# Vision tower kernel: part of VectorE's set-up stands behind the first pixel sums

## The reference

```
x_new = s*x - dt*s*a*z + dt*s*Bu
z_new = dt*s*x + s*z + dt*dt*s*Bu
```

## Time and profile before

| | us |
|---|---|
| median of three runs | 881.12 |
| the three runs | 879.34, 881.12, 882.15 |
| the profiled execution | 881.01 |
| its span in the trace | 879.2 |

### The profile page before, as it was taken

How to read it: one execution, slowest core, us unless ns; L and a number is a source line. 1 busy time by engine, 2 the same in 40 slices (tenths; PEclk the granted TensorE clock), 3 DMA queues, 4 the chain that set the end, 5 groups by cost and what they waited for, 6 DMA issues and landing times.

```text
span 879.2 us, 23479 instructions
## 1 busy us (share of the span) xinstructions
PE 838.2 (95%) x9144; PEld 360.6 (41%) x9144; DVE 717.9 (82%) x1189; ACT 483.5 (55%) x782; POOL 524.4 (60%) x387
## 2 busy tenths in 40 slices
PE   5799999999999999999999997898999999999996
PEld 2134334344344343343343443464444444444442
DVE  5788888888888888888888888894788788788785
ACT  3646456455454464564554554358666566566562
POOL 2699999999999999999999964101121121121110
PEclk9999999999999999999999998999999999999999
DMA  9588998989989989999899764000000000000000
GB/s 374 158 240 252 260 283 245 263 267 260 275 250 260 286 242 259 278 250 263 256 253 264 217 168 111 2 2 2 0 13 13 25 13 13 25 13 13 25 13 36
DMA packets 70560, 141.60 MB, mean 161 GB/s; under 512 B 5440, under 2 KB 5440, under 8 KB 69440
## 3 DMA queue, kind: packets, MB, share of 16 engines
q1 hardware_dynamic: 70464, 140.21, 55.4%
HBM read 68.88 MB, written 4.19 MB: 83 GB/s over the span
## 4 chain that ended last, share of the span: by engine, by line
PE 39%; POOL 37%; issue 7%; DVE 7%; ACT 4%; DMA 3%; SPq 2%; POOLq 1%; DVEq 0%; ACTq 0%
POOL sb_rows L497 11%; POOL sb_prodv L604 7%; POOL sb_rows L502 6%; PE ring L1207 5%; POOL sb_wgt L592 4%; PE ring L1177 4%; POOL sb_rows L504 3%; POOL sb_score L586 3%; PE ring L952 3%; PE bank_ms L1219 3%; DMA sb_wbc<-sb_wgt 3%; SPq L545 2%; PE bank_ms L924 2%; PE qp L991 2%; PE qp L1162 2%
## 5 line engine op out<-in xcount | busy, mean ns | idle before, releaser
L952 PE MATMUL ring<-sb_arena,sb_wqkv 64*64 64x512 f32 x2048 | 254.1, 599 | 2.3 <-DVE sb_prodk L1349 1.5
L1380 DVE TENSOR_TENSOR sb_prodv<-ring,sb_wbc 128x1024 f32<-128x1024 f32 x128 | 151.8, 1206 | 43.6 <-DMA sb_wbc<-sb_wgt 25.4
L1349 DVE TENSOR_TENSOR sb_prodk<-ring,sb_qbuf 128x1024 f32<-128x1024 f32 x128 | 150.6, 1218 | 22.3 <-PE ring L952 16.8
L648 POOL TENSOR_TENSOR sb_parts_q<-sb_arena,sb_const 128x512 fp32r<-128x512 f32 x15 | 15.6, 1039 | 245.6 <-DVE sb_arena L1585 194.4
L497 POOL TENSOR_TENSOR sb_rows<-sb_arena 128x2048 f32<-128x2048 f32 x31 | 142.2, 4586 | 15.8 <-DVE sb_sum L489 15.8
L692 ACT ACTIVATE sb_xsq<-sb_arena 128x2048 f32<-128x2048 f32 x64 | 118.6, 1901 | 2.0 <-DMA sb_arena<-x 2.0
L952 PEld LDWEIGHTS ring<-sb_arena,sb_wqkv 64*64 64x64 f32 x2048 | 66.3, 132 | 115.6 <-issue 72.3
L991 PEld LDWEIGHTS qp<-sb_prodv,sb_tok_w 64*64 64x64 f32 x3072 | 93.1, 137 | 40.4 <-issue 40.2
L991 PE MATMUL qp<-sb_prodv,sb_tok_w 64*64 64x128 f32 x3072 | 98.8, 276 | 5.2 <-POOL sb_prodv L604 5.2
L604 POOL TENSOR_TENSOR sb_prodv<-sb_prodv 128x256 f32<-128x256 f32 x128 | 92.8, 735 | 10.7 <-DVE sb_prodv L1380 10.7
L663 ACT ACTIVATE sb_means<-sb_sum 128x256 f32<-128x256 f32 x32 | 13.3, 416 | 146.9 <-POOL sb_sum L507 143.1
(11 more groups left out here) (248 smaller groups left out, 1450.1 us busy)
## 6 DMA issues: line engine op xcount, KB each, us to landing
sb_arena<-x SPq DMA_DIRECT2D x64, 1024.0 KB, 7.4
sb_wbc<-sb_wgt SPq DMA_DIRECT2D x256, 256.0 KB, 5.7
out<-sb_arena SPq DMA_DIRECT2D x16, 256.0 KB, 2.0
sb_rest_w<-rest_w SPq DMA_DIRECT2D x1, 950.5 KB, 21.3
sb_const<-const SPq DMA_DIRECT2D x1, 264.5 KB, 3.0
sb_tok_w<-tok_w SPq DMA_DIRECT2D x1, 260.5 KB, 2.9
sb_const<-const SPq DMA_DIRECT2D x1, 256.0 KB, 21.6
```

The costliest lines, as they stand in the source:

```text
L952: mm = pe.matmul(ring[slot][C * half:C * half + C, i, :], image_block(w, i), x[C * i:C * i + C, m, half, c], start=True, stop=True)
L1349: dve.tensor_tensor(by_pixel(prodk[:, c]), by_pixel(ring[c % 2][:, :, :]), q[:, :, None, :].to_broadcast([P, 2, N_PIX, G32]), ALU.mult).th ...
L1380: dve.tensor_tensor(prodv[:, :, :, G32 * c:G32 * (c + 1)], by_pixel(ring[k % 2][:, :, :]), by_pixel(wbc[:, c]), ALU.mult).then_inc(values_ ...
```

## The change

On DVE, `double_steps(1)` and `double_steps(2)` stay where they are. `double_steps(4)`, `double_steps(8)` and the six small operations go from in front of the two bias operations to behind the second half of the first pixel sums. Nothing is added or taken out, and no other engine's program changes.

```diff
-            for k in (1, 2, 4, 8):
+            for k in (1, 2):
+                double_steps(k)
+            dve.wait_ge(setup_mm, 2)
+            dve.tensor_copy(bqkv[:, 1:2], banks[1][:, 1:2]).then_inc(biases_ready, 1)
+            dve.tensor_scalar(bqkv[:, 0:1], banks[1][:, 0:1], float(C) ** -0.5, None, ALU.mult).then_inc(biases_ready, 1)
+
+            first_patch_sums(dve, 0)
+            dve.wait_ge(setup_mm, 3)
+            dve.tensor_tensor(bqkv[:, 2:3], banks[2][:, 0:1], vec(V_PROJB), ALU.add).then_inc(weights_scaled, 1)
+            first_patch_sums(dve, 1)
+
+            for k in (4, 8):
                 double_steps(k)
             link(dve.tensor_scalar(svc(SV_F), svc(SV_S), DT * DT, None, ALU.mult))
             link(dve.tensor_tensor(svc(SV_FB), svc(SV_F), vec(V_BB), ALU.mult))
...
             link(dve.tensor_scalar(svc(SV_G), svc(SV_S), 1.0, None, ALU.add))
             link(dve.tensor_tensor(svc(SV_G), svc(SV_G), svc(SV_NM), ALU.add))
             assert n_coefs[0] == N_COEFS
-            dve.wait_ge(setup_mm, 2)
-            dve.tensor_copy(bqkv[:, 1:2], banks[1][:, 1:2]).then_inc(biases_ready, 1)
-            dve.tensor_scalar(bqkv[:, 0:1], banks[1][:, 0:1], float(C) ** -0.5, None, ALU.mult).then_inc(biases_ready, 1)
-
-            first_patch_sums(dve, 0)
-            dve.wait_ge(setup_mm, 3)
-            dve.tensor_tensor(bqkv[:, 2:3], banks[2][:, 0:1], vec(V_PROJB), ALU.add).then_inc(weights_scaled, 1)
-            first_patch_sums(dve, 1)
```

## The result

| | before | changed |
|---|---|---|
| median of 15 runs, us | 880.80 | 884.42 |
| lowest and highest | 878.81 to 882.73 | 880.96 to 890.60 |
| profiled execution, us | 881.01 | 885.80 |
| its span | 879.2 | 884.0 |

The ratio is 1.0047, with a 95% interval of 1.0032 to 1.0062: the kernel became slower by 0.47%, where 0.3% faster was forecast. Ratios and their intervals aren't quotients of medians (1.0041 here) and can differ from them by about 0.001. The changed kernel also scatters more, over 9.6 us against 3.9.

A forecast was written before the change was run, and what follows sets the result against it. In the first 36 us the filling of the pipeline counts, with DVE's set-up the path; later PE and POOL are near full. From span 879.20, minus 2.68, plus 1.81, rebased to the median: 878.4; eight in ten 876.7 to 880.6.

The forecast's parts named there:

- What comes forward on DVE: DVE's set-up and first pixel sums: L1318 starts at 7.77, L483 waits for data until 8.00; sums 2.68 us earlier.
- rival (b): Transfers of x are the limit: landing 1 us later loses 0.8 to 1.0, giving 879.3; chance 0.12.
- The place is an idle stretch of 3.12 us, the block is 2.77, so it costs nothing: Behind DVE's pixel sums: moved block runs 13.43 to 16.20, hidden by the wait for ACT, 0.36 to spare; nothing charged.
- POOL wins 0.8 and it costs nothing downstream: POOL's first instruction, limited by unit 1's second half landing at 15.5, gains 0.8 us; its reader ACT isn't delayed.
- TensorE's clock: PE's slow first pixel-mean matmuls: stretch moved, not changed, taken as 0; bounds 0.36 won or 1.3 lost.
- Rival (c): PE stays at the low rate from its new start to unit 1's squares: loss 6.7, ending at 885.1; chance 0.03.
- All behind 27 us is the same sequence, displaced: Behind 27 us no clock of its own is left: everything follows 2.68 us earlier, full stages neither stretching nor absorbing it.
- Rival (d): Moved block on DVE isn't hidden, later slots late by 0.36 and again 1 us: 879.4; chance 0.05.

The follow-up runs named there:

- experiment 5: Changed kernel, with DVE's six small operations also waiting for unit 1's pixels, as POOL's first instruction does, tensor inputs kept: 886.54, ratio 1.0072.
- 6: Changed kernel, DVE's six small operations also wait for unit 1's pixels; FB, CD and G take their second input as per-partition scalar: 880.56, ratio 1.0000.
- 7: Kernel before plus eight unused 128x512 DVE instructions of several forms, placed beside POOL's first instruction and again where POOL waits: one execution, 892.33.
- 2: Changed kernel, but POOL's first instruction (pixel sums of unit 1) also waits for the last coefficient: 878.82, ratio 0.9977.
- Experiment 10: Kernel before with five additional unused one-input reductions of 128x1024 on DVE behind the pixel sums: 883.89, ratio 1.0047.
- 11: Changed kernel, the six small operations behind the sums in one-input form, doublings for 4 and 8 in front of unit 0's score_scale: 878.75, ratio 0.9983.
- experiment 8: Changed kernel, DVE's six small operations also wait for unit 1's pixels, and PE computes unit 0's mean squares four times: 886.22, ratio 1.0058.
- experiment 1: Changed kernel, same order, with FB, CD and G taking their second input as a per-partition scalar: 879.38, ratio 0.9983.

## Why the prediction was wrong

- *What comes forward on DVE*: right to 0.1 us in the profiled execution, in part by luck. L483 was to wait for the transfer until 8.00; the first half of x landed 0.5 earlier (ACT at 7.52), DVE's set-up ran 0.09 later, and L483 started at 8.00 with no wait. The 2.68 was the value of one landing; on the average of the 14 it is 2.1. I had named this as rival (b) and given it 0.12, as an event; it is a distribution that the old kernel hid.
- *The place is an idle stretch of 3.12 us, the block is 2.77, so it costs nothing*: this step failed. The block ends at 21.97 and not at 16.20. I carried durations from a place where POOL was idle (it had nothing before 16.27) to one where POOL works, and counted only whether DVE was free. Half the reason stood in the prediction: POOL's L497 comes 0.8 us forward, to 15.5, and the block reaches to 16.20. I asked what that meant for POOL's readers and not for its neighbour. In the first 16 us the trace of before couldn't show the price, since the sums' end released POOL: DVE's two-input instructions were over when POOL began. But it shows the hold near the end of the tokenizer, on another line with two tensor inputs (the lines stand below this list): beside POOL's L597 the first L1398 takes 1.09 us instead of 0.48 and ends 0.28 behind it. The longest and the shortest time of each DVE instruction over the whole span would have given the warning. Experiments 5, 6 and 7 show the mechanism, 2 that its removal brings the gain back.
- *POOL wins 0.8 and it costs nothing downstream*: POOL started at 15.02, its sums ended at 24.1, and nobody waited for them. True, and beside the point.
- *TensorE's clock*: bounded at 1.3 us on the assumption that PE's idle time ahead of each stretch stays as it was. With DVE late PE was idle for 7.14 us, and 0.8 to 2.8 more were lost in the executions profiled where the low rate followed. Rival (c) had a loss of rate and, with 885.1, almost the measured time, but that is luck: it put the loss down to the full rate not coming at all, and in the changed kernel the full rate was there (keys at 14.95 in 1.90, squares at 16.77 in 1.92) until PE had to wait. Experiment 10 shows that lateness alone brings the loss.
- *All behind 27 us is the same sequence, displaced*: right. The displacement at unit 2's L497 is 5.4 (41.67 against 36.30) and at unit 6's 5.5; the full stage neither stretched nor absorbed it. The sign of what was displaced was wrong.
- Rival (d), the block isn't hidden, had the right place with a price of 1 us and a chance of 0.05. It took the block's length for safe; its price should have been the length of the POOL instructions beside it, 4.53 and 2.34.

The hold in the trace of the kernel before, first beside POOL, then alone:
```profile
534.12 1.28 POOL L597 TENSOR_TENSOR sb_wgt<-sb_wgt,sb_srz 128x512 f32<-128x512 f32 x1
534.59 1.09 DVE L1398 SCALAR_TENSOR_TENSOR sb_arena<-sb_arena,sb_sv 128x256 f32<-128x256 f32 x1
...
538.76 0.48 DVE L1398 SCALAR_TENSOR_TENSOR sb_arena<-sb_arena,sb_sv 128x256 f32<-128x256 f32 x1
```

## What to carry to other kernels

Before moving small DVE work into DVE's idle time, look at POOL in the same stretch: an instruction with two tensor inputs in on-chip memory, however narrow, or a wide multiplication by a scalar, may last as long as the POOL instruction that it meets. A reduction (0.62) and a memset (0.48) ran undisturbed, and so did products that read one of their inputs from PSUM, where PE's results lie: two of L1349 took 2.36 us beside POOL's L502 and L504 in the kernel before, and two of L1352 the same 2.36 without POOL in the changed one. If a transfer decides when POOL starts, the meeting is a matter of chance: order the two by a semaphore, as in 2, or put the work where POOL waits anyway, as in 11.

## What else the runs showed

- The first half of x lands over a range of 2.7 us between executions (6.95 to 9.65), unit 1's likewise (POOL released from 14.48 to 17.14). One profile gives one draw of it; a slack of 0.2 us against a transfer is no slack.
- PE at the 1.2 GHz level behind 7 us of idle time: keys 3.69 us instead of 2.22 for 16 matmuls, scores 3.46 instead of 1.92, granted clock 0.50 from 25 to 30 us. Behind 2.35 us of idle time the level fell as well, somewhat later (experiment 8). A longer wait doesn't mean a longer slow stretch: behind 4.42 us of idle time keys and scores were both slow (experiment 1, 3.69 and 3.64), behind 6.98 us only the keys (experiment 5, 3.53 and 1.92).
